# Four-block transformer-like chain on one core: the token-mixing product as 64x64 blocks in four corners of TensorE, placed behind the own-token products

## The reference

```python
x = x + (einsum('bsi,bio->bso', x, W[id]) + b[id])          # an expert per sample
x = x + (x @ W.T + lora(x, A[adapter], Bm[adapter]))        # one matrix, rank-16 delta
x = x + attention(x, ...)   # 8 heads, window of 256 keys out of a paged cache, own 64 tokens written into it
w = weights[subjects]       # (64, 64, 64): one 64x64 matrix per sample, 8 subjects
x = x + einsum('bct,bcd->bdt', x, w) + bias[subjects][:, :, None]
```

## Time and profile before

| | us |
|---|---|
| median of three runs (992.5 to 996.27) | 994.13 |
| the profiled execution, its own time | 993.04 |
| its span, from the first to the last instruction | 991.2 |
| TensorE busy | 938.0 (95%) |
| VectorE / ScalarE / GpSimd busy | 600.8 / 385.4 / 514.6 |
| phase one, phase two | to about 510, about 521 to 991 |
| a pair of steps of phase two | about 14.1 |

### The profile page before, as it was taken

The page is one execution under the profiler, slowest core; times in us unless marked ns, Lnnn a source line. Parts: engine busy times, 40 slices in busy tenths (PEclk is TensorE's granted clock), DMA queues, the critical chain, the costliest instruction groups (busy, mean ns, idle before and its releaser), DMA issues.

```text
span 991.2 us, 22128 instructions
## 1 busy us (share of the span) xinstructions
PE 938.0 (95%) x6253; PEld 679.9 (69%) x6253; DVE 600.8 (61%) x1788; ACT 385.4 (39%) x1061; POOL 514.6 (52%) x469
## 2 busy tenths in 40 slices
PE   6899999999999999999976999999899999899997
PEld 4576766766766767667665777777677777677775
DVE  5334434656656544357554767777677677676775
ACT  2122121221221221222225656565565656565653
POOL 1345555355464477653565555555455555555530
PEclk9999999999999999999999999999999999999999
DMA  9779887777668767687456565656565666556641
GB/s 313 267 255 314 299 276 267 242 236 272 237 231 274 232 239 263 216 279 258 151 183 177 155 194 165 196 175 191 155 189 181 182 199 198 168 176 195 199 134 45
DMA packets 105162, 212.48 MB, mean 214 GB/s; under 512 B 29563, under 2 KB 52056, under 8 KB 96930
## 3 DMA queue, kind: packets, MB, share of 16 engines
q1 hardware_dynamic: 71042, 145.54, 43.4%
q0 software_dynamic: 25088, 57.74, 19.7%
q10 hardware_dynamic: 8992, 8.73, 2.8%
HBM read 204.39 MB, written 33.86 MB: 240 GB/s over the span
## 4 chain that ended last, share of the span: by engine, by line
PE 90%; issue 2%; DVE 2%; another core or an unknown queue 2%; ACT 2%; DMA 1%; SPq 1%; ACTq 0%; DVEq 0%
PE banks L589 11%; PE banks L755 10%; PE banks L803 10%; PE banks L707 9%; PE banks L791 7%; PE banks L628 6%; PE banks L636 6%; PE banks L638 6%; PE banks L778 4%; PE banks L732 3%; PE banks L839 3%; PE banks L697 3%; PE banks L712 3%; PE banks L796 2%; PE banks L599 2%
## 5 line engine op out<-in xcount | busy, mean ns | idle before, releaser
L548 POOL DMA_INDIRECT ring<-new_rows,idx x128 | 131.0, 1023 | 86.5 <-DVE big L1280 31.0
L460 POOL TENSOR_TENSOR rms<-ss,neg_half 128x12 f32<-128x12 f32 x31 | 70.9, 2286 | 180.7 <-DVE ss L1185 180.7
L931 ACT ACTIVATE big<-big,neg_max 128x320 f32<-128x320 f32 x256 | 141.5, 555 | 3.1 <-DVE neg_max L1243 2.5
L1243 DVE CUSTOM_DVE_ANT_0 big<-banks,mask 128x320 f32<-128x320 f32 x256 | 114.6, 485 | 14.6 <-PE banks L755 10.8
L755 PE MATMUL banks<-kt,q_in 64*128 64x192 f32 (+2 forms) x768 | 103.0, 366 | 20.0 <-remote 10.6
L589 PE MATMUL banks<-ring 128*64 128x512 f32 x512 | 117.1, 599 | 3.1 <-DMA ring<-in_w 3.1
L872 ACT ACTIVATE x2t_hi<-banks 128x512 fp32r<-128x512 f32 x32 | 19.1, 598 | 235.6 <-PE banks L599 235.6
L755 PEld LDWEIGHTS banks<-kt,q_in 64*128 64x128 f32 x768 | 78.8, 188 | 43.2 <-remote 14.1
L501 POOL DMA_INDIRECT ring<-in_kvrows,idx x64 | 61.2, 957 | 60.5 <-PE banks L755 42.8
L921 ACT ACTIVATE kt<-banks 128x384 f32<-128x384 f32 x128 | 61.9, 484 | 74.1 <-PE banks L733 52.6
L589 PEld LDWEIGHTS banks<-ring 128*64 128x64 f32 x512 | 33.9, 136 | 81.5 <-issue 79.4
(11 more groups left out here) (169 smaller groups left out, 2011.6 us busy)
## 6 DMA issues: line engine op xcount, KB each, us to landing
ring<-in_w SPq DMA_DIRECT2D x62, 1024.0 KB, 5.9
ring<-in_xt SPq DMA_DIRECT2D x32, 256.0 KB
x_in<-in_x SPq DMA_DIRECT2D x32, 256.0 KB, 5.5
bias_in<-in_b SPq DMA_DIRECT2D x64, 128.0 KB, 5.4
x_dram<-x SPq DMA_DIRECT2D x32, 256.0 KB, 4.9
q_dram<-q_t ACTq DMA_DIRECT2D x32, 256.0 KB
new_rows<-kv_out SPq DMA_DIRECT2D x32, 256.0 KB, 4.7
q_in<-q_dram SPq DMA_DIRECT2D x64, 128.0 KB
```

Of the source, the lines that this page charges most:

```text
L548: pool.indirect_dma_start(out=kv[:, s, c, :], out_offset=None, in_=new_rows, in_offset=bass.IndirectOffsetOnAxis(ap=idx[:, b, 1 + c:2 + c] ...
L931: nc.scalar.activation(prob[:, s % 2, PLACE[g] * NK:(PLACE[g] + 1) * NK], sm[:, s % 2, g, :], ACT.Exp, bias=neg_max[:, s % 2, g:g + 1], sc ...
L1243: V.tensor_tensor_reduce(sm[:, s % 2, g, :], ps_s[g], mask[:, s % 2, k0:k0 + NK], 1.0, 3.0e38, ALU.add, ALU.min, accum_out=neg_max[:, s % ...
```

## The change

The mixing product becomes four products for a pair, each of a 64x64 matrix and `x3[64, 256]`: row half h of the array holds the matrix of sample h of the pair, column half i of the array takes the columns of half i of the 512. Sample h's result lies in its own bank (`ps_mix[h]`: bank 7, and the right half of bank 6, whose left half takes L771's transposes), with the column halves one above the other in the partitions. The identity is added to the eight matrices once, in phase one, and they are stored as `mixing` in DRAM; so the sum with `x3` falls away. The biases of all samples are computed once into `sbias[128, 64]`. ScalarE, no longer VectorE, adds the bias (two operations of 128x256) at the head of the odd step. The product stands behind `values()`; the waits for the pair's loads and `x3_ready` stand ahead of `values()`. L771's transposes of an odd step wait for `x4_ready`. `x4` goes out with two DMAs of 1 KB rows.

```diff
+        mixing = nc.dram_tensor("mixing", (NS, T, T), F32).ap()
-        bd = sb("bd", [P, 2, P])
-        sbias = sb("sbias", [P, 2, 1])
+        w3 = sb("w3", [P, 2, T])
+        w3_all = sb("w3_all", [P, NS // 2, T])
...
-        ps_last, ps_mix = ps[0:2], ps[2:4]
+        ps_last, ps_mix = ps[0:2], (ps[7][:, 0:D // 2], ps[6][:, GP * P:2 * GP * P])
...
-            sp.wait_ge(pool_set, 3)
+            sp.wait_ge(mixing_ready, 1)
+            for h in range(2):
+                sp.dma_start(mixing[h * NS // 2:(h + 1) * NS // 2].rearrange("n c d -> c n d"), w3_all[T * h:T * h + T, :, :]).then_inc(
+                    st_mixing, 16)
+            sp.wait_ge(h_done, NP)
+            sp.wait_ge(qkv_done, NP)
...
-                        sp.dma_start(bd[T * h:T * h + T, t, T * h:T * h + T],
-                                     a["w3"][bass.ds(u, 1)].rearrange("o c d -> (o c) d")).then_inc(ld_pair[t], 16)
-                        sp.dma_start(sbias[T * h:T * h + T, t, :],
-                                     a["b3"][bass.ds(u, 1)].rearrange("o d n -> (o d) n")).then_inc(ld_pair[t], 16)
+                        sp.dma_start(w3[T * h:T * h + T, t, :], mixing[bass.ds(u, 1)].rearrange("o c d -> (o c) d")).then_inc(ld_pair[t], 16)
...
-            nc.gpsimd.memset(bd[:, :, :], 0.0).then_inc(pool_set, 1)
...
                     pe.wait_ge(prob_ready, G * b)
+                    if s % 2 == 1 and on(b, 5, NB):
+                        pe.wait_ge(x4_ready, pair)
...
                     pe.wait_ge(ld_pair[pair_s], PAIR_DMAS * 16 * (j * 2 + s // 4))
-                    for i, (n0, n1) in enumerate(COLUMN_PARTS if is_last(pair) else WHOLE):
-                        pe.wait_ge(x3_ready, pair + 1 + i)
-                        nc.tensor.matmul((ps_mix[i] if is_last(pair) else ps_x)[:, n0:n1], bd[:, pair_s, :], x3[:, pair_s, n0:n1],
-                                         start=True, stop=True).then_inc(l3_done, 1)
-                if on(b, 1, NB) and not behind_probs:
+                    pe.wait_ge(x3_ready, pair + 1)
+                    if not behind_probs and on(b, 1, NB):
+                        values()
+                    if is_last(pair):
+                        pe.wait_ge(x4_ready, pair)
+                    for i, (n0, n1) in enumerate(COLUMN_PARTS):
+                        if i == 1 and is_last(pair):
+                            pe.wait_ge(x3_ready, pair + 2)
+                        for h in range(2):
+                            last = nc.tensor.matmul(ps_mix[h][T * i:T * i + T, :], w3[T * h:T * h + T, pair_s, :],
+                                                    x3[T * h:T * h + T, pair_s, n0:n1], start=True, stop=True, skip_group_check=True)
+                        if i == 1 or is_last(pair):
+                            last.then_inc(l3_done, 1)
+                elif on(b, 1, NB):
                     values()
...
+                if s % 2 == 1 and on(b, 5, NB):
...
+                        for h in range(2):
+                            last = nc.scalar.activation(x4[rows, pair_s, D // 2 * h:D // 2 * (h + 1)], ps_mix[h][rows, :], ACT.Identity,
+                                                        bias=sbias[rows, bass.ds(pair * 2 + h, 1)])
+                        last.then_inc(x4_ready, 1)
...
+            def subject_bias():
+
+                link(V.tensor_scalar(sbias[:, :], subject[:, :], 0, bias_col[:, 0:1], ALU.is_equal, ALU.mult))
+                for n in range(1, NS):
+                    link(V.tensor_scalar(sbias_one[:, :], subject[:, :], n, bias_col[:, n:n + 1], ALU.is_equal, ALU.mult))
+                    link(V.tensor_tensor(sbias[:, :], sbias[:, :], sbias_one[:, :], ALU.add))
+                dve.wait_ge(ld_mixing, 32)
+                for h in range(2):
+                    rows = slice(T * h, T * h + T)
+                    link(V.tensor_tensor(w3_all[rows, :, :], w3_all[rows, :, :],
+                                         ident[rows, rows].unsqueeze(1).to_broadcast([T, NS // 2, T]), ALU.add))
...
+            SIDE = {2: take_tables, NP - 8: subject_bias, ROW_STEP: make_rows, NP - 1: take_indices}
...
-                        V.scalar_tensor_tensor(x4[:, pair_s, n0:n1], (ps_mix[i] if is_last(pair) else ps_x)[:, n0:n1], sbias[:, pair_s, 0:1],
-                                               x3[:, pair_s, n0:n1], ALU.add, ALU.add).then_inc(x4_ready, 1)
```

More of the change, by code:

```diff
@@ L226, in build @@
         TOK_PARTS = 4
-        PAIR_DMAS = 5
+        PAIR_DMAS = 3
         def loop(eng, step, slots, first, end, last):
@@ L394, in phase_two @@
                     k, t = (b // 2 if isinstance(b, int) else j * 2 + s // 2) - 3, 1 - s // 2
-                    for i, (n0, n1) in enumerate(COLUMN_PARTS if is_last(k) else WHOLE):
-                        sp.wait_ge(x4_ready, k + 1 + i)
-                        sp.dma_start(a["out"][bass.ds(k, 1), :, n0:n1].rearrange("o p d -> (o p) d"), x4[:, t, n0:n1]).then_inc(st_out[t], 16)
+                    for i, (n0, n1) in enumerate(COLUMN_PARTS):
+                        if i == 0 or is_last(k):
+                            sp.wait_ge(x4_ready, k + 1 + i)
+                        sp.dma_start(a["out"][bass.ds(k, 1), :, n0:n1].rearrange("o (h c) n -> c (o h) n", h=2),
+                                     x4[T * i:T * i + T, t, :].rearrange("c (h n) -> c h n", h=2)).then_inc(st_out[t], 16)
                 if s % 2 == 0 and on(b, 2, NB):
@@ L401, in phase_two @@
                     wait(sp, x4_ready, k - 1)
+                    if isinstance(k, int) and k == 0:
+                        sp.wait_ge(st_mixing, 32)
                     sp.dma_start(x2_in[:, t, :], x2_dram[bass.ds(k, 1)].rearrange("o p d -> (o p) d")).then_inc(ld_pair[t], 16)
@@ L943, in copy_own @@
                     nc.scalar.activation(pt2[:, :, :].rearrange("p q t -> p (q t)"), ps_pt2[:, 0:GP * P], ACT.Copy).then_inc(pt2_ready, 1)
+                if s % 2 == 1 and on(b, 5, NB):
+                    pair, pair_s = (b // 2 if isinstance(b, int) else j * 2 + s // 2) - 2, s // 2
+                    wait(act, st_out[pair_s], 2 * 16 * (j - 1))
+                    for i in range(2 if is_last(pair) else 1):
+                        rows = slice(T * i, T * i + T) if is_last(pair) else slice(0, P)
+                        act.wait_ge(l3_done, pair + 1 + i)
+                        for h in range(2):
+                            last = nc.scalar.activation(x4[rows, pair_s, D // 2 * h:D // 2 * (h + 1)], ps_mix[h][rows, :], ACT.Identity,
+                                                        bias=sbias[rows, bass.ds(pair * 2 + h, 1)])
+                        last.then_inc(x4_ready, 1)
                 if on(b, -1, NB):
@@ L1095, in take_indices @@
                 V.tensor_copy(idx[:, :, 3], tview[:, 2, 1, :]).then_inc(idx_ready, 1)
+            def subject_bias():
[4 more added lines that the diff above has]
+                dve.wait_ge(ld_mixing, 32)
+                for h in range(2):
+                    rows = slice(T * h, T * h + T)
+                    link(V.tensor_tensor(w3_all[rows, :, :], w3_all[rows, :, :],
+                                         ident[rows, rows].unsqueeze(1).to_broadcast([T, NS // 2, T]), ALU.add))
+                V.tensor_copy(scol[:, 8:9], scol[:, 3:4]).then_inc(mixing_ready, 1)
             def rotate_last(k, r):
@@ L1248, in phase_two @@
                     masked(0)
-                if finished:
-                    wait(dve, st_out[pair_s], 16 * (j - 1))
-                    for i, (n0, n1) in enumerate(COLUMN_PARTS if is_last(pair) else WHOLE):
-                        dve.wait_ge(l3_done, pair + 1 + i)
-                        dve.wait_ge(x3_ready, pair + 1 + i)
-                        V.scalar_tensor_tensor(x4[:, pair_s, n0:n1], (ps_mix[i] if is_last(pair) else ps_x)[:, n0:n1], sbias[:, pair_s, 0:1],
-                                               x3[:, pair_s, n0:n1], ALU.add, ALU.add).then_inc(x4_ready, 1)
                 if on(b, 0, NB):
```

34 lines of the change are left out of this document (20 added, 14 removed).

## The result

The changed kernel takes 1013.58 us (median; 1006.78 to 1019.63), the one before 994.75 in the same comparison: a ratio of 1.0179, 95% interval 1.0131 to 1.0228. It is slower, as forecast, but by 18.8 us where 10 were forecast, and the time lies above the range (980 to 1011). The profiled execution took 1019.63 us, 1017.8 of it span, at the upper end of its own runs.

What follows compares the result with a forecast made beforehand. The prediction took GpSimd's gathers, holding TensorE's releases, to bound even steps and TensorE's own order odd ones. From the profiled 993.04 us, +10.7 for x4 and -0.5 at the ends gave 1003.2, 1004 against the median; range 980 to 1011.

Steps and rivals of the forecast that it cites:

- The gathers' hold: Even steps: TensorE's releases are held back while GpSimd issues the gathers L548, and some 0.65 us beyond.
- the mixing product's gain hidden behind it: Even step: the cheaper mixing product's gross gain, 0.45 us a pair, doesn't show because the chain of gathers ends last.
- the two releases at 759.68 and 759.70: End of the even step: TensorE's last scores piece and ScalarE's `ot_hi`, held-back releases said to come 0.04 us apart.
- The mixing product, 0.6 us: TensorE, even step: four corner products with 256 columns take 0.6 us (0.45 to 0.76) instead of 1.05.
- Its new place, cost 0: Even step, product behind the values: TensorE waits 0.7 us for ScalarE's copy, scores start 0.24 later, covered by slack.
- x4 on ScalarE, 0.37 a pair: Transposes L771 wait for ScalarE's two operations behind `ot_hi`: 0.37 us lost a pair, +10.7 us over 29 pairs.
- VectorE's gain 0: VectorE loses the sum L1255, 0.75 us, which waited for nothing and kept nobody waiting: gain 0.
- DMAs and ends: Five transfers a pair instead of six: 0, bounds -0.5 and +1; last even steps without a gather: -0.5 us.
- Phase one, 0 and at worst 0.7 us: Phase one's bias table and matrix sums, some 5 us of work, fit the step's 7 us: 0, at worst 0.7.
- backlog: Rival: late releases are the mixing product's own backlog and shrink with it; 977 us, or 986 for half; chance 0.2.
- ot_hi through a gap: Rival: `ot_hi` slips through a gap in the hold and x4 follows at once; no change, 994 to 996 us; chance 0.15.
- corners that don't overlap: Rival: the four corners don't overlap in pairs of banks, product 2.1 us; 1045 us; chance 0.05, with similar new waits.

Runs made afterwards that it cites:

- e4: The kernel before without the second gather L548 (odd rows of new tokens missing from the result): ratio 0.952, 47 us faster.
- h2: The changed kernel with a 224-byte unused tile ahead of `ring` and the mixing product back ahead of the values, x4 still on ScalarE: ratio 1.0141.
- h1: The changed kernel with a 224-byte unused tile ahead of `ring`, which puts it on a multiple of 256 bytes: ratio 1.0105.
- e1: The kernel before with only the change's preparations added (matrices, bias table, DRAM table, wider inputs), phase two untouched: ratio 1.007, 7 us slower.
- f2: The kernel before with one unused tile of 32 bytes a partition ahead of `ring`: ratio 1.0067, 6.7 us slower.
- f1: The same kernel as h1 in an earlier comparison, the changed kernel with the 224-byte unused tile: ratio 1.0138.

## Why the prediction was right and wrong

- **The gathers' hold, and the mixing product's gain hidden behind it: right**, by e4 (no second gather, no stall) and by the stall of 0.64 us in h2. One reading was off: the two releases at 759.68 and 759.70 are 0.02 us apart, not 0.04; nothing hangs on it.
- **The mixing product, 0.6 us: right** (0.55 to the next instruction).
- **Its new place, cost 0: right for the change as made**, since undoing it alone gave no faster kernel (h2 against h1), and for the even step (5.76 with it and without). Once x4 is split, undoing it is worth 4.8 us, of which I had none. TensorE waited 1.03 us for ScalarE's copy in the step shown, 0.7 forecast, still inside the slack. In the odd to even part it costs 0.05 us then (8.43 against 8.38).
- **x4 on ScalarE, 0.37 a pair: right in size**, 0.38 by the cut of the pair, of which 0.32 go when x4 is split. A term inside was off: the two operations took 0.84 us from start to end, not 0.64; the transposes started 0.09 behind them, where I had 0.15. From ot_hi to the transposes it is 1.21 us in the step shown, 0.78 before: 0.43 more, where the chain that I worked out gave 0.28. That I took 0.37, between 0.3 and the bound of 0.5, is partly luck.
- **VectorE's gain 0: right.** Its busy time didn't fall by 23 us, though, it rose by 5.6: phase one gives it 22.7 more, 6.0 of them the bias table's, 10.8 in the masked sums of the merge, the same 96 instructions as before. ScalarE's rose by 25.8 us and not by 19, since an x4 operation took 471 ns where I had 365.
- **DMAs and ends:** nothing in the runs separates them.
- **Phase one, 0 and at worst 0.7 us: this step failed.** I priced the new instructions and found them hidden, which they nearly are: 0.6 to 1.2 us in their step, and nothing to be told between e1 and f2. I didn't ask what the wider inputs and the two new tiles do to the place of everything declared behind them. The shift costs 6.7 us by f2 (4.2 to 9.3); with the 10.5 us of h1 that is 17.2 of the 18.8 us measured. By f1, the same kernel as h1, it would be 20.4, so the sum holds to some 3 us.
- **The rivals:** backlog falls with e4; ot_hi through a gap and corners that don't overlap with the trace after. The one that came about, a slower phase one, wasn't among them, and so my range ended at 1011.

## What to carry to other kernels

A new tile or a wider one moves all that is allocated behind it: compare the start of every tile that a DMA writes, modulo 256 bytes, before pricing the change (0 and 32 are the two values measured here). When an engine's releases are held by another's transfers, the time saved under the hold isn't there to be had, and moving the transfers moves the hold; measure a period in parts, since one part can gain what the other loses, and look at its mean beside its median, since pairs that take turns hide in medians. A wait that the profile doesn't name can be found in the timeline as an end on one engine followed at once by a start on another.

## What the runs showed of the hardware that I had not expected

- 32 unused bytes ahead of the tiles that DMAs write made packets of 8192 bytes 6% slower (374 to 396 ns; 4%, 378 to 394, over the longer stretch), those of 512 bytes 17% (35 to 41), and the kernel 0.67%.
- Work that stands in the same place grows when another engine's moves beside it: VectorE's 96 masked sums took 38.1 us before, 48.9 in the changed kernel and 50.1 in f2, which has nothing but the 32 bytes. In f2 GpSimd, late from its wait for the loads, runs beside them:

```profile
192.19 1.69 POOL L451 TENSOR_TENSOR x_in<-x_in,bias_in 128x512 f32<-128x512 f32 x1 [2.51 <-DMA ring<-in_rope]
192.65 1.81 DVE L1044 CUSTOM_DVE_ANT_0 later<-same,stage 128x320 f32<-128x320 f32 x1
...
195.70 0.72 DVE L1044 CUSTOM_DVE_ANT_0 later<-same,stage 128x320 f32<-128x320 f32 x1
```

Of the 48 sums proper (the other 48 instructions read the accumulator), those that overlap a GpSimd TENSOR_TENSOR for less than a third of their time take 710 to 715 ns on average in each of the eighteen traces; the others, where there are any, 1240 to 1360. Before there is none of the slow ones, in the changed kernel there are 20, in f2 21. What of this reaches the kernel's time no run separates.
